# Chunk 0's row tiles shared with GpSimd, the lane one-hots on ScalarE, chunk 2's convolution off VectorE, and a new table of places, in a fused Mamba and mixture-of-experts layer

## The chip, the core and the metric

The kernel runs on one core of a Trainium2 chip. A core has TensorE (PE, matrix multiply), VectorE (DVE), ScalarE (ACT), GpSimd (POOL) and SyncE (SP, which here only issues DMAs). Each engine works through its own list of instructions in order; semaphores tie the lists together. The metric is the device time of one launch in microseconds (us), the median of three runs. A measurement of this kernel tells changes of about 0.2% (2.5 us) from none.

## The reference

The input is 4 sequences of 1024 tokens with 256 features, all float32. It is normalized by a layernorm to `xn`, and three things are added: the input, a Mamba block of `xn`, and a mixture of experts of `xn`.

```
xn    = layernorm(x)
# Mamba: 512 channels, 16 states
rn    = xn * rsqrt(mean(xn^2) + eps) * norm_w
skip, x_in = rn @ skip_w.T, rn @ in_w.T
x     = silu(conv_b + sum_k x_in[t-3+k] * conv_w[:, k])          # 4 taps in time
delta = softplus(x @ wd1.T @ wd2.T + wd2_b)
h[t]  = exp(delta[t] * A) * h[t-1] + delta[t] * x[t] * B[t]      # per channel and state
y[t]  = sum_n h[t, :, n] * C[t, n] + x[t] * W_D
mamba = xn + (y * silu(skip)) @ out_w.T
# experts: the 2 of 8 with the LOWEST gate are used for each token
gates = softmax(xn @ Wr); scores of the two, normalized to sum 1
ffn   = sum_e score_e * ((silu(xn @ W1[e]) * (xn @ V1[e])) @ W2[e])
out   = x + mamba + ffn
```

## The kernel before

**Tiling.** The 4096 tokens are cut into 16 chunks of 256 (`CHUNKS`); four chunks make a sequence. In a chunk the recurrence over time is done state by state: a unit `w` is one chunk, one half `q` of the 512 channels and one of the 16 states, so a chunk has 32 units and the kernel 512. For each unit ACT makes two decays `aexp` (`exps`, L557), DVE makes the product of delta, x and B (`bps`, L1149) and runs two scans along time (`hb`, L1170), and for each pair of units POOL multiplies the states by C (`part`, L775) and PE adds them up over the states by transposing into one accumulator (`yps`, L870). C and B rows come broadcast from DRAM (`bcr`, SP). DVE also saves the last state of each scan (`carry`, L1158). At the start of each half chunk ACT copies x into `ups` (`fill_ups`, L566), and DVE multiplies it by delta (L1142).

**Pieces and places.** All other work is cut into pieces, and a table says in which unit of which chunk each piece stands (`pieces`, `B_PLACES`, `O_PLACES`, `F_PLACES`); `LATER` moves a kind of piece some units back on one engine. Every engine does, in each unit `w`, its own part of the unit and then its part of the pieces at `w`. ACT makes the decays two units ahead (`EXP_AHEAD`). A piece that must wait holds everything behind it on that engine. Pieces that matter here:
- `B1`, `B2`, `CV`/`CW`, `X2`, `B3`, `B4`, `B5`, `SP`, `DL`: the next chunk's x, convolution, delta, and B and C rows. The convolution is either on DVE (`DVE_CONV`, L1294 and L1298) or as `CV` on ACT (four scaled copies, L617 and L619) and `CW` on POOL (two additions, L805 and L807). `DL`, one addition of 128x1024, is on DVE (`DVE_DELTA`) or on POOL. `O1` to `O3`: the end of the chunk before (DVE L1305).
- `R`, 18 pieces in chunk 0: the row tiles. For each pair of the 32 tiles of 128 tokens, ACT writes the normalized rows into one of two buffer pairs `tok` (L688), SP stores them, POOL writes the residual (L797), PE transposes the rows of the pair before (L1006), ACT copies them out of the banks (L694), and PE multiplies the pair before that with the router (L998).
- `RA` to `RE`: the router's softmax, choice and placement, mostly on DVE, one instruction after another. They need all of `R`.
- `M`, 8 rounds in chunk 1: from the slot of each token the lists of the experts' tiles are built. Each round DVE makes a one-hot of the tile (L1279) and one of the lane within it (`hot`, 8 rows of 128, L1282), POOL multiplies (L815, L817), PE adds up 8 products in bank X (L1020). DVE may not overwrite a buffer of two rounds ago before PE has read it (`placed`).
- `MF`: DVE turns bank X into the index list (L1332 to L1336). `FB` -1: POOL gathers the rows of the first two tiles by it (L783), PE transposes the first (L1050), ACT copies it (L715). Then `FA`, `FB`, `FC` are the steps of each of the 71 expert tiles, in chunks 2 to 15: DVE L1340 and L1348, PE L1033, L1057, L1067.

Of the kernel before, what the change touches and what calls it, by code (L numbers as in the profile page):

```python
# [22 lines left out]
P = 128  # L23
# [36 lines left out]
    "other": [4, 6, 7, 8, 11, 11, 12, 14, 14, 16, 16, 18, 21, 23, 23, 24, 25, 26, 26],  # L60
# [5 lines left out]
    1: [1, 4, 4, 11, 18],  # L66
    14: [3, 3, 3, 15, 18],
    15: [0, 0, 6, 7, 15],
# [6 lines left out]
    "five": [1, 6, 8, 10, 13, 15, 16, 16, 17, 19, 20, 28, 29, 29, 30],  # L75
    "six": [0, 0, 5, 9, 10, 11, 11, 14, 15, 17, 17, 19, 26, 26, 28, 29, 29, 31],
# [4 lines left out]
    "router": [8, 8, 8, 9, 9, 9],  # L81
# [4 lines left out]
DVE_CONV = (0, 2)  # L86
# [3 lines left out]
DVE_DELTA = (0, 2)  # L90
# [60 lines left out]
def carry_copies(w):  # L151
# [74 lines left out]
def mamba_moe(nc, x, norm_w, skip_wT, in_wT, conv_w, conv_b, wd1T, wd2T, wd2_b, wBCT, A_log, W_D, out_wT,  # L226
# [3 lines left out]
    with ctx:  # L230
# [132 lines left out]
        added = sem("added")  # L363
        hot_set = sem("hot_set")
# [11 lines left out]
        y_taken = sem("y_taken")  # L376
        xn_r = sem("xn_r")
# [56 lines left out]
        def _(sp):  # L434
# [19 lines left out]
            def do(piece):  # L454
# [17 lines left out]
                elif kind == "R" and piece[1] < TT // 2:  # L472
# [4 lines left out]
                    sp.wait_ge(xn_r, 2 * (i + 1))  # L477
# [5 lines left out]
                elif kind == "R" and piece[1] == TT // 2:  # L483

                    sp.dma_start(v1[:, :].rearrange("p (e k f) -> p e k f", e=EXPERTS, k=KD), V1.rearrange("e (k p) f -> p e k f", p=P)).then_inc(ld_v1, 16)
                    sp.wait_ge(xn_r, TT)
# [50 lines left out]
        def _(act):  # L537
# [38 lines left out]
            def do(piece):  # L576
# [102 lines left out]
                elif kind == "R":  # L679
                    i = piece[1]  # L680
                    if i < TT // 2:
                        if i == 0:
                            act.wait_ge(stat, STAT_LN[1])
                        if i >= 2:
                            wait_full(act, "V", ("R", i - 1))
                            act.wait_ge(xt_out[i % 2], 16 * (i // 2))
                        for t in (2 * i, 2 * i + 1):
                            nc.scalar.activation(tok[:, t % 4, :], xall[:, t, :], ACT.Identity, bias=nm2[:, 0, t:t + 1],  # L688
                                                 scale=rs2[:, 0, t:t + 1]).then_inc(xn_r, 1)
                    if 1 <= i <= TT // 2:  # L690
                        for k, t in enumerate((2 * i - 2, 2 * i - 1)):
                            wait_full(act, "HV"[k], piece)
                            at_least(act, lgt, t - 1)
                            nc.scalar.activation(xT[:, k, :, :], bank["HV"[k]][:, 0:D].rearrange("p (k t) -> p k t", k=KD),  # L694
                                                 ACT.Copy).then_inc(free["HV"[k]], 1)
                elif kind == "RA":
# [58 lines left out]
        def _(pool):  # L755
# [30 lines left out]
            def do(piece):  # L786
                kind = piece[0]
                if kind == "R" and piece[1] < TT // 2:
                    i = piece[1]
                    if i == 0:  # L790
                        pool.wait_ge(stat, STAT_LN[1])
                        for k in range(TT // 8):
                            pool.wait_ge(ld_x[k], 16)
                    at_least(pool, res_out[i % 2], 16 * (i // 2))
# [64 lines left out]
        def _(pe):  # L859
# [30 lines left out]
            def do(piece):  # L890
# [99 lines left out]
                elif kind == "R":  # L990
# [10 lines left out]
                    if 1 <= i <= TT // 2:  # L1001
                        for k, t in enumerate((2 * i - 2, 2 * i - 1)):
                            wait_free(pe, "HV"[k], piece)
                            pe.wait_ge(xn_r, t + 1)
# [82 lines left out]
        def _(dve):  # L1087
# [184 lines left out]
            def value_rows(r):  # L1272
# [7 lines left out]
                if r == 0:  # L1280
                    dve.wait_ge(ones_set, 2)
                v.tensor_tensor(hot[r % 2], steps.unsqueeze(1).to_broadcast([P, ROUND, P]),  # L1282
                                lane[:, at].unsqueeze(2).to_broadcast([P, ROUND, P]), ALU.is_equal).then_inc(hot_set, 1)
# [130 lines left out]
```

## Time and profile before

| | us |
|---|---|
| median of 3 runs (1269.9 to 1270.19) | 1269.93 |
| the profiled execution's own time | 1272.05 |
| its span, first to last instruction | 1270.2 |
| DVE busy in the span | 1173.1 (92%) |
| PE, ACT, POOL busy | 1076.9, 1010.5, 998.2 |
| first scan of chunks 0, 1, 2, 3, 4 starts at | 40.8, 126.4, 246.3, 323.8, 395.4 |

Busy time is the sum over an engine's instructions. The later chunks take about 72 us each; chunk 0 takes 85 us and chunk 1 120 us. "Idle before" in a row is what an engine stood still before the instruction, and the name behind the arrow is what ended it.

### The profile page before, as it was taken

How to read it: one execution, taken by the hardware profiler on the slowest of the kernel's cores; microseconds unless marked ns; L12 is line 12 of the kernel's file. 1: busy time of each engine (PE TensorE's matmuls, PEld its weight loads, DVE VectorE, ACT ScalarE, POOL GpSimd, SP SyncE). 2: the span in 40 equal slices, each digit the busy share in tenths (PEclk: the TensorE clock that was granted, in tenths of full speed). 3: DMA queues.
4: the chain of work that ended last, by engine and by line, in shares of the span. 5: the costliest groups of instructions: out<-in, count | busy, mean ns of one | idle time of the engine just before them, and what ended most of it. 6: DMA issues, size and time to landing. Idle time of an engine off the chain costs nothing.

```text
span 1270.2 us, 20047 instructions
## 1 busy us (share of the span) xinstructions
PE 1076.9 (85%) x5406; PEld 806.6 (64%) x5406; DVE 1173.1 (92%) x2128; ACT 1010.5 (80%) x2151; POOL 998.2 (79%) x601
## 2 busy tenths in 40 slices
PE   4378576498898989999999999999999999998776
PEld 3266475365666666676767766676766667675664
DVE  5976899989999899999999999999999999999896
ACT  4898346379888897889888898889889898987853
POOL 1487176667898988889898998889899898988764
PEclk8686778798999999999999999999999999998977
DMA  7467822644445454555545454555545455544536
GB/s 229 154 200 227 312 82 82 203 162 130 142 141 153 135 148 153 145 149 137 149 133 161 134 161 139 147 148 131 155 139 157 142 150 150 147 134 132 135 128 191
DMA packets 87117, 195.08 MB, mean 154 GB/s; under 512 B 11184, under 2 KB 47152, under 8 KB 86928
## 3 DMA queue, kind: packets, MB, share of 16 engines
q1 hardware_dynamic: 69008, 171.18, 40.7%
q0 software_dynamic: 17712, 22.55, 10.9%
q8 instruction: 47, 0.77, 0.2%
q14 instruction: 62, 0.51, 0.1%
q10 hardware_dynamic: 288, 0.07, 0.0%
HBM read 171.22 MB, written 26.48 MB: 156 GB/s over the span
## 4 chain that ended last, share of the span: by engine, by line
PE 31%; POOL 29%; ACT 14%; issue 13%; DVE 11%; DMA 1%; POOLq 0%; DVEq 0%; ACTq 0%
POOL part L775 15%; PE yps L870 7%; POOL acc L831 5%; POOL tap L805 4%; ACT aexp L557 4%; PE bankX L1067 4%; PE bankH L1033 4%; PE bankV L1057 4%; DVE hb L1170 3%; PE bankG L910 3%; POOL scr L783 2%; ACT L557 2%; DVE bps L1149 2%; PE bankV L910 2%; POOL x L807 2%
## 5 line engine op out<-in xcount | busy, mean ns | idle before, releaser
L775 POOL TENSOR_TENSOR part<-hb,bcr 128x1024 f32<-128x1024 f32 x256 | 618.3, 2429 | 172.4 <-DVE hb L1170 141.2
L1170 DVE TENSOR_TENSOR_SCAN hb<-aexp,carry,bps 128x256 f32<-128x256 f32 x768 | 545.5, 734 | 4.2 <-ACT aexp L557 4.1
L557 ACT ACTIVATE aexp<-delta,Am 128x256 f32<-128x256 f32 x1024 | 446.8, 501 | 53.0 <-DVE hb L1170 42.0
L870 PE MATMUL yps<-idn,part 128*128 128x128 f32 x2048 | 299.8, 286 | 74.1 <-POOL part L775 64.0
L1149 DVE TENSOR_TENSOR bps<-ups,bcr 128x512 f32<-128x512 f32 x512 | 345.8, 675 | 3.4 <-DMA bcr<-brows 2.3
L870 PEld LDWEIGHTS yps<-idn,part 128*128 128x128 f32 x2048 | 249.9, 147 | 151.2 <-POOL part L775 83.0
L1170 DVE TENSOR_TENSOR_SCAN hb<-aexp,bps 128x256 f32<-128x256 f32 x256 | 167.3, 673 | 10.8 <-ACT aexp L557 10.2
L1067 PE MATMUL bankX<-w,scr 128*128 x568 | 138.7, 388 | 10.5 <-ACT scr L715 8.1
L1033 PE MATMUL bankH<-w,scr 128*128 x284 | 136.8, 604 | 2.2 <-issue 1.0
L1057 PE MATMUL bankV<-v,scr 128*128 x284 | 134.2, 595 | 1.2 <-ACT xin L610 0.8
L831 POOL DMA_INDIRECT acc<-scr,idx x71 | 114.2, 1609 | 24.6 <-issue 11.5
L1067 PEld LDWEIGHTS bankX<-w,scr 128*128 128x128 f32 x568 | 105.6, 194 | 28.1 <-issue 15.6
L805 POOL TENSOR_TENSOR tap<-tap 128x512 f32<-128x512 f32 x56 | 84.7, 1513 | 1.0 <-ACT tap L619 1.0
L783 POOL DMA_INDIRECT scr<-xt,idx x71 | 72.2, 1016 | 13.8 <-issue 7.9
L1033 PEld LDWEIGHTS bankH<-w,scr 128*128 128x128 f32 x284 | 50.3, 193 | 40.1 <-issue 39.2
L619 ACT ACTIVATE tap<-xin,cw 128x256 f32<-128x256 f32 x168 | 72.5, 497 | 0.0
L1057 PEld LDWEIGHTS bankV<-v,scr 128*128 128x128 f32 x284 | 48.4, 190 | 36.5 <-issue 35.9
L1340 DVE SCALAR_TENSOR_TENSOR scr<-scr,bankH 128x512 f32<-128x512 f32 x71 | 47.6, 671 | 22.5 <-ACT scr L705 22.5
L557 ACT ACT_TABLE_LOAD x50 | 64.2, 1283 | 0.9
L705 ACT ACTIVATE scr<-bankH 128x512 f32<-128x512 f32 x71 | 41.7, 587 | 28.8 <-PE bankH L1033 28.5
L725 ACT ACTIVATE scr<-bankX,meta 128x256 f32<-128x256 f32 x71 | 33.1, 466 | 38.3 <-PE bankX L1067 38.3
L1040 PEld LDWEIGHTS bankG<-idn,scr 128*128 128x128 f32 x284 | 35.4, 141 | 37.4 <-issue 36.9
(179 smaller groups left out, 1625.1 us busy)
## 6 DMA issues: line engine op xcount, KB each, us to landing
bcr<-brows SPq DMA_DIRECT2D x256, 512.0 KB
w<-in_W SPq DMA_DIRECT2D x2, 4096.0 KB, 22.1
xch<-in_x SPq DMA_DIRECT2D x16, 256.0 KB, 4.5
w<-in_x SPq DMA_DIRECT2D x4, 1024.0 KB, 9.7
xt<-scr SPq DMA_DIRECT2D x16, 256.0 KB, 3.0
acc<-scr SPq DMA_DIRECT2D x16, 256.0 KB, 2.8
v<-in_V SPq DMA_DIRECT2D x1, 4096.0 KB, 16.0
acc<-mst POOLq DMA_DIRECT2D x15, 256.0 KB
```

Source lines behind the costliest of these rows:

```text
L557: nc.scalar.activation(aexp[:, w % EXP_SLOTS, i, :], delta[:, c % 2, e, :], ACT.Exp, scale=Am[:, e, n:n + 1]).then_inc(s_a, 1)
L619: ins = nc.scalar.activation(tap[:, w, :], xin[:, e, w:w + CH], ACT.Copy, scale=cw[:, e, w:w + 1])
L775: nc.gpsimd.tensor_tensor(part[:, slot:slot + 2, :, :], hb[:, state:state + 2, :, :], bcr[:, row:row + 2, CH:2 * CH].unsqueeze(2).to_broad ...
L783: nc.gpsimd.indirect_dma_start(out=tok[:, j % 2, :], out_offset=None, in_=xt, in_offset=bass.IndirectOffsetOnAxis(ap=idx[:, j:j + 1], axis ...
L805: nc.gpsimd.tensor_tensor(tap[:, 0:2, :], tap[:, 0:2, :], tap[:, 2:4, :], ALU.add).then_inc(cvs, 1)
L831: nc.gpsimd.indirect_dma_start(out=acc, out_offset=bass.IndirectOffsetOnAxis(ap=idx[:, j:j + 1], axis=0), in_=tok[:, 2 + j % 2, :], in_off ...
L870: mm = pe.matmul(yps[:, s, i * P:(i + 1) * P], part[:, w % (2 * PART_PAIRS), i, s * P:(s + 1) * P], idn[:, :], start=(n == 0 and s == 0 an ...
L1033: mm = pe.matmul(bank["H"][:, :], xT[:, j % 2, k, :], w1[:, bass.ds(col + k * FF, FF)], start=(k == 0), stop=(k == KD - 1))
L1057: mm = pe.matmul(bank["V"][:, :], xT[:, j % 2, k, :], v1[:, bass.ds(columns[j] + k * FF, FF)], start=(k == 0), stop=(k == KD - 1))
L1067: mm = pe.matmul(bank["X"][:, 0:D], gT[:, k * P:(k + 1) * P], w2[:, bass.ds(columns[j] + k * D, D)], start=(k == 0), stop=(k == FF // P - 1))
L1149: v.tensor_tensor(bps[w % 2][:, :, :], ups[:, :, :], bcr[:, w % (2 * ROW_PAIRS), 0:CH].unsqueeze(1).to_broadcast([P, 2, CH]), ALU.mult).th ...
L1170: v.tensor_tensor_scan(hb[:, w % STATE_SLOTS, i, :], aexp[:, w % EXP_SLOTS, i, :], bps[w % 2][:, i, :], first, ALU.mult, ALU.add).then_inc ...
```

## The change

Three kinds of work move, and the tables of places and of `LATER` have new numbers.
- Of each pair of row tiles ACT normalizes the even one as before, and POOL the odd one, by one `tensor_scalar`, before it writes the residual of the pair. A new semaphore `xn_p` counts POOL's tiles beside `xn_r`; PE and SP wait for both.
- The lane's one-hots are no longer made by one comparison on DVE. ACT makes each round by eight activations `Abs(lane - step)` of 128x128 and, once these are done (`far_set`), one `Relu(1 - ...)` of 128x1024. ACT now waits for the end of the router (`STAT_END`) and for `placed`.
- Chunk 2's convolution goes to ACT (`CV`) and POOL (`CW`), and its `DL` to POOL. Only chunk 0 keeps them on DVE.

```diff
@@ tables (a line or two of each) @@
-    1: [7, 7, 8, 8, 9, 12, 12, 14, 14, 16, 16, 17, 20, 20, 22, 22, 22, 22, 25],
+    1: [6, 6, 8, 9, 9, 9, 11, 11, 11, 11, 12, 15, 21, 22, 22, 22, 27, 27, 27],
...
-    1: [2, 4, 6, 8, 14, 20, 22, 24, 29, 30],
+    1: [2, 4, 6, 8, 10, 20, 22, 24, 31, 31],
...
-    "router": [8, 8, 8, 9, 9, 9],
+    "router": [8, 8, 8, 8, 8, 8],
...
-DVE_CONV = (0, 2)
+DVE_CONV = (0,)
...
-DVE_DELTA = (0, 2)
+DVE_DELTA = (0,)
@@ ScalarE @@
-                        for t in (2 * i, 2 * i + 1):
-                            nc.scalar.activation(tok[:, t % 4, :], xall[:, t, :], ACT.Identity, bias=nm2[:, 0, t:t + 1],
-                                                 scale=rs2[:, 0, t:t + 1]).then_inc(xn_r, 1)
+                        t = 2 * i
+                        nc.scalar.activation(tok[:, t % 4, :], xall[:, t, :], ACT.Identity, bias=nm2[:, 0, t:t + 1],
+                                             scale=rs2[:, 0, t:t + 1]).then_inc(xn_r, 1)
...
+                elif kind == "M":
+                    r = piece[1]
+                    if r == 0:
+                        act.wait_ge(stat, STAT_END)
+                        act.wait_ge(ones_set, 2)
+                    if r >= 2:
+                        act.wait_ge(placed, r - 1)
+                    for k in range(ROUND):
+                        at = r * ROUND + k
+                        ins = nc.scalar.activation(hot[r % 2][:, k, :], steps, ACT.Abs, bias=lane[:, at:at + 1], scale=-1.0)
+                    ins.then_inc(far_set, 1)
+                    act.wait_ge(far_set, r + 1)
+                    nc.scalar.activation(hot[r % 2], hot[r % 2], ACT.Relu, bias=1.0, scale=-1.0).then_inc(hot_set, 1)
@@ GpSimd @@
+                    if i >= 2:
+                        wait_full(pool, "V", ("R", i - 1))
+                        pool.wait_ge(xt_out[i % 2], 16 * (i // 2))
+                    t = 2 * i + 1
+                    nc.gpsimd.tensor_scalar(tok[:, t % 4, :], xall[:, t, :], rs2[:, 0, t:t + 1], nm2[:, 0, t:t + 1],
+                                            ALU.mult, ALU.add).then_inc(xn_p, 1)
@@ TensorE @@
-                            pe.wait_ge(xn_r, t + 1)
+                            pe.wait_ge((xn_r, xn_p)[k], t // 2 + 1)
@@ VectorE @@
-                if r == 0:
-                    dve.wait_ge(ones_set, 2)
-                v.tensor_tensor(hot[r % 2], steps.unsqueeze(1).to_broadcast([P, ROUND, P]),
-                                lane[:, at].unsqueeze(2).to_broadcast([P, ROUND, P]), ALU.is_equal).then_inc(hot_set, 1)
```

ACT's list in chunk 1, behind the router, before the change: from the silu of `O2` 1 (y<-bankV) to the copy of chunk 0's output (mst).

```order
L668 ACTIVATE y<-bankV 128x512
L557 ACT_TABLE_LOAD
L557 ACTIVATE aexp<-delta,Am 128x256 x6
L587 ACTIVATE xch<-xch,nm,rs 128x256 x2
L593 ACTIVATE rnT<-bankG,nw 128x256 x2
L557 ACTIVATE aexp<-delta,Am 128x256 x2
L607 ACTIVATE xin<-xin 128x4x3
L610 ACTIVATE xin<-bankG 128x2x256
L557 ACTIVATE aexp<-delta,Am 128x256 x4
L610 ACTIVATE xin<-bankV 128x2x256
L557 ACTIVATE aexp<-delta,Am 128x256 x2
L678 ACTIVATE mst<-bankH 128x256
```

The end of the same stretch with the change (w<-w are the one-hots' parts, tap<-xin the convolution's `CV`; its lines are numbered a little higher).

```order
L709 ACTIVATE w<-w 128x128 x8
L712 ACTIVATE w<-w 128x1024
L561 ACTIVATE aexp<-delta,Am 128x256 x2
L621 ACTIVATE tap<-xin,cb,cw 128x256
L623 ACTIVATE tap<-xin,cw 128x256 x3
L561 ACTIVATE aexp<-delta,Am 128x256 x2
L614 ACTIVATE xin<-bankV 128x2x256
L709 ACTIVATE w<-w 128x128 x8
L712 ACTIVATE w<-w 128x1024
L561 ACTIVATE aexp<-delta,Am 128x256 x2
L621 ACTIVATE tap<-xin,cb,cw 128x256
L623 ACTIVATE tap<-xin,cw 128x256 x3
```

Up to this copy ACT now has five rounds of one-hots and all four `CV` in its list, between the same decays; it had none of either.

DVE's list around the index list (`MF`: meta and idx) at the end of chunk 1, before the change.

```order
L1332 COPY meta<-bankX 128x71
L1334 TENSOR_SCALAR w<-bankX,idb 128x71
L1336 CAST idx<-w 128x71
L1170 SCALAR_TENSOR_TENSOR hb<-aexp,carry,bps 128x256
L1149 TENSOR_TENSOR bps<-ups,bcr 128x512
L1170 SCALAR_TENSOR_TENSOR hb<-aexp,carry,bps 128x256
L429 TENSOR_TENSOR delta<-delta,y 128x1024
L1158 TENSOR_REDUCE carry<-hb 128x4
L1170 SCALAR_TENSOR_TENSOR hb<-aexp,carry,bps 128x256
L1142 TENSOR_TENSOR ups<-ups,delta 128x512
```

And with the change.

```order
L1193 SCALAR_TENSOR_TENSOR hb<-aexp,carry,bps 128x256
L1165 TENSOR_TENSOR ups<-ups,delta 128x512
L1172 TENSOR_TENSOR bps<-ups,bcr 128x512
L1193 SCALAR_TENSOR_TENSOR hb<-aexp,carry,bps 128x256
L1351 COPY meta<-bankX 128x71
L1353 TENSOR_SCALAR w<-bankX,idb 128x71
L1355 CAST idx<-w 128x71
```

`MF` stood before the last two units of chunk 1 and now stands behind them; `DL` is gone from the list.

## Rows read from the trace of the kernel before

**Rows 1.** Busy time by stage: window, length, PE, PEld, DVE, ACT, POOL busy, clock, DMA.

```profile
49.30:108.40 59.10, 43.98 (x256) 37.08 (x256) 50.27 (x97) 56.27 (x130) 49.12 (x41) 0.80 0.60 195
108.40:131.30 22.90, 20.32 (x93) 18.72 (x94) 7.74 (x13) 16.79 (x39) 12.65 (x15) 0.54 0.73 240
...
155.70:237.20 81.50, 53.53 (x300) 46.58 (x300) 81.03 (x134) 42.30 (x83) 56.58 (x30) 0.82 0.28 86
237.20:264.40 27.20, 15.08 (x62) 11.22 (x62) 19.98 (x35) 12.03 (x24) 12.48 (x7) 0.69 0.80 262
```

**Rows 2.** DVE's waits from 49.3 to 131.3 us: total, times, longest.

```profile
DVE ups L1142 <- ACT ups L566: 10.4, 2, 9.5
DVE hb L1170 <- ACT aexp L557: 8.5, 6, 2.0
```

**Rows 3.** ACT in order of time, chunk 0: start, length in us, instruction.

```profile
53.76 1.08 ACT L688 ACTIVATE scr<-w,nm,rs 128x256 f32<-128x256 f32 x2
54.75 0.36 ACT L694 ACTIVATE scr<-bankH 128x256 f32<-128x256 f32 x1
...
58.19 0.60 ACT L617 ACTIVATE tap<-xin,cb,cw 128x256 f32<-128x256 f32 x1
...
59.90 1.08 ACT L688 ACTIVATE scr<-w,nm,rs 128x256 f32<-128x256 f32 x2
```

**Rows 4.** POOL's residual writes, 49.3 to 131.3 us: busy us, mean ns.

```profile
L797 POOL TENSOR_SCALAR scr<-w,r,nm 128x256 f32<-128x256 f32 x32 | 17.5, 558 | 7.6 <-DMA acc<-scr 5.1 <-DVE r L1130 2.5
```

**Rows 5.** PE in order of time, the last row tiles.

```profile
109.81 1.47 PE L998 MATMUL bankX<-wrt,scr 128*128 128x8 f32 x8 [3.09 <-ACT scr L694]
...
126.03 1.87 PE L998 MATMUL bankX<-wrt,scr 128*128 128x8 f32 x8
129.49 1.72 PE L998 MATMUL bankX<-wrt,scr 128*128 128x8 f32 x8
```

**Rows 6.** DVE in order of time, between the router's two halves.

```profile
140.60 0.43 DVE L1215 TENSOR_TENSOR w<-w 128x256 f32<-128x256 f32 x1
...
143.26 0.42 DVE L1224 COPY w<-bankV 128x256 f32<-128x256 f32 x1
```

**Rows 7.** DVE's groups from 155.7 to 246.3 us: busy us, mean ns.

```profile
L1282 DVE TENSOR_TENSOR w<-w 128x1024 f32<-128x1024 f32 x8 | 9.7, 1215 | 0.0
...
L1298 DVE SCALAR_TENSOR_TENSOR x<-xin,cw,x 128x256 f32<-128x256 f32 x12 | 5.8, 485 | 0.4
L1294 DVE TENSOR_SCALAR x<-xin,cw,cb 128x256 f32<-128x256 f32 x4 | 3.3, 825 | 0.0
```

**Rows 8.** ACT in order of time, two activations of `B4` and one of `SP`.

```profile
215.21 0.47 ACT L650 ACTIVATE delta<-bankH,db 128x256 f32<-128x256 f32 x1
215.57 0.48 ACT L648 ACTIVATE y<-bankH,db 128x256 f32<-128x256 f32 x1
...
219.64 1.04 ACT L657 ACTIVATE y<-y 128x1024 f32<-128x1024 f32 x1
```

**Rows 9.** ACT's decays, 155.7 to 237.2 us: busy, mean ns, idle before.

```profile
L557 ACT ACTIVATE aexp<-delta,Am 128x256 f32<-128x256 f32 x52 | 22.9, 500 | 30.8 <-DVE hb L1170 30.7
```

**Rows 10.** ACT's waits for PE in that window, first and last of seven.

```profile
ACT mst L678 <- PE bankH L957: 6.3, 1, 6.3
...
ACT y L648 <- PE bankH L936: 0.5, 1, 0.5
```

**Rows 11.** DVE, then PE, in order of time, from the index list on.

```profile
237.65 2.12 DVE L1336 CAST idx<-w 128x71 int32<-128x71 f32 x1
...
248.11 0.66 PE L1050 MATMUL bankX<-idn,scr 128*128 128x128 f32 x2 [11.49 <-DMA scr<-xt,idx]
253.28 3.78 PE L1033 MATMUL bankH<-w,scr 128*128 x4
```

**Rows 12.** DVE in order of time, its last long wait in chunk 2.

```profile
300.18 0.69 DVE L1340 SCALAR_TENSOR_TENSOR scr<-scr,bankH 128x512 f32<-128x512 f32 x1 [2.70 <-ACT scr L705]
```

**Rows 13.** DVE's longest waits in total, 395.4 to 1117.6 us.

```profile
DVE scr L1340 <- ACT scr L705: 11.6, 13, 1.8
```

More of the change, by code:

```diff
@@ L56 @@
 B_PLACES = {
[3 rows of a table removed]
-    "other": [4, 6, 7, 8, 11, 11, 12, 14, 14, 16, 16, 18, 21, 23, 23, 24, 25, 26, 26],
[3 rows of a table added]
+    "other": [4, 6, 7, 9, 11, 11, 13, 14, 15, 17, 17, 18, 21, 23, 23, 23, 24, 26, 27],
 }
@@ L65 @@
 O_PLACES = {
-    1: [1, 4, 4, 11, 18],
-    14: [3, 3, 3, 15, 18],
-    15: [0, 0, 6, 7, 15],
+    1: [1, 3, 4, 12, 19],
+    14: [3, 3, 4, 10, 20],
+    15: [0, 0, 5, 6, 11],
     "other": [3, 3, 3, 15, 19],
@@ L71 @@
 F_PLACES = {
[3 rows of a table removed]
-    "five": [1, 6, 8, 10, 13, 15, 16, 16, 17, 19, 20, 28, 29, 29, 30],
-    "six": [0, 0, 5, 9, 10, 11, 11, 14, 15, 17, 17, 19, 26, 26, 28, 29, 29, 31],
[3 rows of a table added]
+    "five": [0, 7, 8, 11, 13, 15, 16, 16, 17, 19, 20, 28, 29, 29, 31],
+    "six": [0, 0, 5, 8, 8, 11, 11, 14, 15, 17, 17, 19, 26, 26, 28, 29, 29, 30],
     15: [17, 21, 29, 29, 31],
@@ L363, in mamba_moe @@
         added = sem("added")
+        far_set = sem("far_set")
         hot_set = sem("hot_set")
@@ L376, in mamba_moe @@
         y_taken = sem("y_taken")
+        xn_p = sem("xn_p")
         xn_r = sem("xn_r")
@@ L476, in do @@
                         sp.dma_start(xt[TOKENS:TOKENS + P, :], empty).then_inc(xt_zero, 16)
-                    sp.wait_ge(xn_r, 2 * (i + 1))
+                    sp.wait_ge(xn_r, i + 1)
+                    sp.wait_ge(xn_p, i + 1)
                     sp.dma_start(xt[2 * i * P:2 * (i + 1) * P, :].rearrange("(s p) d -> p s d", p=P),
@@ L485, in do @@
                     sp.dma_start(v1[:, :].rearrange("p (e k f) -> p e k f", e=EXPERTS, k=KD), V1.rearrange("e (k p) f -> p e k f", p=P)).then_inc(ld_v1, 16)
-                    sp.wait_ge(xn_r, TT)
+                    sp.wait_ge(xn_r, TT // 2)
+                    sp.wait_ge(xn_p, TT // 2)
                     sp.wait_ge(res_set, TT)
```

16 rows, old and new, of tables (B_PLACES, F_PLACES, LATER) are left out of this document.

## The prediction

> **What bounds the kernel now.** I read the profile in this order: busy time by stage, DVE's waits, and then the lists of ACT, POOL and PE in order of time in the stretches that the change touches. From chunk 3 on DVE is the bound: it has 64 scans and 32 products in every chunk, and from 395 to 1118 us its largest wait comes to 11.6 us [rows 13]. The change leaves that part nearly as it is, so its worth is decided before 324 us, in four stretches with four different bounds.
>
> - 49.3 to 108.4 us, chunk 0 behind the row statistics. ACT is busy 56.3 of 59.1 us, POOL 49.1, DVE 50.3 [rows 1]. DVE waits for decays, 8.5 us in this stretch and the next [rows 2]: ACT is the bound.
> - 108.4 to 131.3, the last eight pieces `R`. Nobody is full in the table [rows 1], and DVE stands 9.5 us before the `ups` of chunk 1 [rows 2], which ACT has behind these pieces. From the first to the last of seven PE steps L998 are 19.68 us, so 3.28 us a piece, of which one L998 alone is 1.87 at a granted clock of 0.54, that is mostly the 1.2 GHz level [rows 1, 5]. The bound is the ring PE, ACT, PE.
> - 131.3 to 155.7 the router, on DVE alone; 155.7 to 237.2 the rest of chunk 1 up to `MF`: DVE busy 81.0 of 81.5, ACT 42.3, POOL 56.6 [rows 1]. ACT stands 30.7 us there because DVE has not scanned [rows 9]. DVE is the bound by a wide margin.
> - 237.2 to 264.4, from the index list to the end of chunk 1's `O1` in chunk 2. DVE is busy 20.0 of 27.2 us. It's a chain: list, gather, PE transpose (PE had stood 11.5 us for it), first expert matmul [rows 1, 11].
>
> **Part 1, the row tiles.** Each pair costs ACT 0.99 us from start to start for two tiles [rows 3], so 0.50 for the one that goes. Ten pairs lie in the first stretch: ACT does 5.0 us less there. POOL does 10 tiles more by 0.558 [rows 4], 5.6 us, and comes to 49.1 + 5.6 = 54.7 us of work, where ACT would come to a length of 59.1 - 5.0 = 54.1: the two are level, and each also waits for the other in the convolution. I take 4.0 of the 5.0 us. In the second stretch the tile taken from ACT is beside the ring and not in it; the copy L694 starts some 0.5 us earlier only where the normalization stood ahead of it. The ring without any ACT tile is 1.87 for L998, about 0.7 for the first transposes and 0.4 for the copy, with hand-overs about 3.1 against 3.28: 7 times 0.15 is 1.0 us. Together -5.0. Bounds: all 16 tiles pay at ACT's price, -8.0; POOL becomes the bound, eats the whole gain and adds its own waits, +1.0.
>
> **Part 2, the router in one piece.** `RP` on PE runs between the router's halves. Before, DVE did a whole unit there: from the end of L1215 at 141.03 to L1224 at 143.26 are 2.2 us [rows 6]. All router pieces now stand in one unit, so DVE stands for these 2.2 us, and the unit is still to be done: +2.2, bounds +1.5 and +2.5.
>
> **Part 3, from the router's end to `O1` in chunk 2.** From DVE go 9.7 us of one-hots and 3.3 + 5.8 of convolution [rows 7], and 1.2 of `DL`. To ACT come four `CV`, 1.71 each from start to start [rows 3], 6.8 us, and eight rounds of one-hots, which the trace doesn't show. Their nearest rows are the activations with a bias column on 256 elements: 0.48 long, but started 0.36 apart [rows 8]. For 128 elements I take starts 0.27 apart; 7 of them, one full length of 0.36 before the semaphore lets go, and 1.04 for the 1024 elements of the `Relu`, as in L657 [rows 8], make 3.3 us a round, 26.4 in all. Bounds: if each of the eight takes its whole length, 0.36 each, and 0.1 for the hand-over, a round is 4.0, and all 32; at starts 0.22 apart it is 24.
>
> ACT then has 42.3 us [rows 1], about 2.5 for the decays of two units more that now stand before `MF` (0.88 a unit [rows 9], and a fill), 26.4 and 6.8: 78. It stood 14.5 us for PE in this window, from 6.3 down to 0.5 [rows 10]; most of that was slack and goes when ACT is late itself, and I keep 5. So ACT needs 83.5 us to where `MF` now stands. DVE needs 81.5 - 9.7 - 9.1 + 3.8 for the two units now ahead of `MF` + 1.4 for `ups` and product, 68: it will wait for decays, above all in units 10 to 14, where five rounds and four `CV` stand in ACT's list. POOL gets four `CW` and `DL`, some 10 us: 56.6 + 10 is still below 83.5, and nothing is on the path. Its own wait for ACT holds `parts` behind it, which has slack of two units.
>
> The Trainium skill (ScalarE: Activation LUTs, Rules for kernel authors) budgets about 0.3 us for each activation with a bias column and 0.83 ns an element. By it a round would be 8 times 0.41 and 1.15, 4.4 us, and the eight 35; the case's activations of 256 elements would be 0.51 apart, and they start 0.36 apart [rows 8], so the rule fits a length and not a rate here.
>
> Behind `MF` the chain of 27.2 us [rows 1] stays, but for the sums of PE that had piled up between its transpose and the first expert matmul, 248.77 to 253.28 [rows 11]: `MF` and the gather now come one piece of PE's list later, POOL's products for these sums are then made while PE waits, and I take 2.5 us off. The list's place behind the last two units costs nothing more in this sum, since it is in the 83.5. So before it was 81.5 + 27.2 = 108.7, and now 83.5 + 24.7 = 108.2: -0.5. The 20 us that leave DVE are thus worth almost nothing: ACT is late in their stead, and the chain has two units less of DVE's work to hide behind. Bounds: DVE as the bound, 68 + 24.7, -16; ACT keeping all its 14.5 us of waits, 93 + 24.7, +9.
>
> **Part 4, the rest.** In chunk 2 `FA` 2 stands two units later, and the wait of 2.7 us before it [rows 12] should mostly go: -1.5. In chunks 3 to 15 the places move by one unit here and there; their waits for this step were 11.6 us in ten chunks [rows 13]: 0, with ±2.5.
>
> **The sum.** -5.0 + 2.2 - 0.5 - 1.5 = -4.8. The profiled execution would go from 1272.05 to 1267.2; it was 2.1 above the median of the runs, so the median goes from 1269.93 to **1265.1**.
>
> **The rivals.**
> - *DVE stays the bound in chunk 1* (rounds near 3.0 and no waits of ACT that matter). For it: 30.7 us in which ACT stood [rows 9]. Against it: 33 us are put in, unevenly. -5.0 + 2.2 - 16 - 1.5: 1250.
> - *POOL becomes the bound in chunk 0* and the tiles only change engines. For it: 54.7 against 54.1, and each `R` of POOL now has three steps, with waits for SP's stores before two of them. The -5.0 becomes -1.0: 1269.
> - *Short activations don't overlap*, a round is 4.0. For it only their length [rows 8]; the skill's rule above points the same way, and further. The rounds cost 5.6 more on the bound: 1270.7.
> - *Slower: ACT's waits in chunk 1 don't shrink.* Place: the copies of PE's results by ACT between the router and `MF`. With one-hots in ACT's list, PE's rounds wait for ACT and ACT for PE, and DVE may not start round r before PE has done r-2. Price: 14.5 in place of 5, part 3 is +9, and the sum +4.7: 1274.6. It decides from about 10 us of such waits on, where the sum passes zero. For it: the list is strict, and PE already waited for POOL's rows before. Against it: a late ACT finds PE done.
>
> **Chances.** My forecast, with its own range 1260.5 to 1267.4, 0.45; DVE-bound 0.12; POOL-bound 0.13; no overlap 0.10; slower 0.20. Within 0.2% means 2.5 us, what can't be told from no change. Faster is 0.45 + 0.12 and a little of the third, 0.58; same 0.22; slower 0.20. The range for 8 in 10 reaches over most of both sides: 1253 to 1275.
>
> **What would show it.** Right: ACT nearly full from 155 us to `MF`; DVE with some 12 us of waits for decays there, in units 10 to 14; rounds of 3.3; 2.2 us of DVE standing inside the router; the router's start 5 us earlier; POOL over 90% busy in chunk 0. Wrong: DVE busy all through chunk 1 (first rival); the router's start at 130 (second); Abs starts 0.36 apart or more (third); ACT standing 10 us for PE in chunk 1 (fourth). A change of more than 3 us behind 324 us would mean that the places of the later chunks matter, which I have put at 0.

## The result and the profile after

The changed kernel takes 1262.03 us (median of 4, 1260.95 to 1263.79), the kernel before 1270.06 on the same chip (median of 4): ratio 0.9931, 95% interval 0.9919 to 0.9944, so 8.0 us or 0.7% faster. The profiled spans are 1259.2 and 1270.2, -11.0. The forecast was 1265.1, faster; the time lies in its own range, 1260.5 to 1267.4. Its sum, -4.8, was smaller than the result, and its terms did not all come true.

The changed kernel by stage, in the columns of [rows 1]: row tiles, last pieces `R`, router's end to `MF`, `MF` to the end of `O1` in chunk 2.

```profile
49.30:107.30 58.00, 43.36 (x252) 37.16 (x252) 49.65 (x96) 51.78 (x120) 51.97 (x50) 0.80 0.64 203
107.30:129.80 22.50, 20.34 (x97) 18.93 (x98) 8.67 (x16) 13.76 (x33) 19.03 (x22) 0.57 0.71 230
152.40:236.80 84.40, 54.64 (x316) 46.38 (x316) 71.92 (x122) 78.12 (x179) 65.35 (x41) 0.80 0.30 95
236.80:258.30 21.50, 12.95 (x58) 10.32 (x58) 12.44 (x25) 9.84 (x19) 10.17 (x6) 0.69 0.90 309
```

Against [rows 1] the first stretch is 1.1 us shorter, the second 0.4, the router 1.8 (22.6 for 24.4, between the windows), the third 2.9 longer and the fourth 5.7 shorter. That is -6.1 at the end of `O1`; -4.9 more come behind it.

- **ACT in the first stretch.** Its work fell by 4.5 us, as forecast, but it is no longer nearly full. ACT's waits, and below PE's, from 49.3 to 107.3 (waiter, releaser; total, times, longest):

```profile
ACT y L652 <- PE bankH L959: 2.3, 1, 2.3
ACT xin L614 <- PE bankG L933: 1.5, 1, 1.5
...
PE yps L893 <- POOL part L792: 5.8, 4, 3.3
```

In the same stretch before, ACT's longest wait for PE was 1.0 and PE's for `part` 1.5 in total. DVE's decays cost 11.8 us and the `ups` 2.9 where [rows 2] had 8.5 and 10.4.

- **The router.** DVE in order of time; the place of [rows 6]:

```profile
139.13 0.43 DVE L1238 TENSOR_TENSOR w<-w 128x256 f32<-128x256 f32 x1
141.82 0.42 DVE L1247 COPY w<-bankV 128x256 f32<-128x256 f32 x1 [2.26 <-PE bankV L1037]
142.28 1.11 DVE L1252 TENSOR_TENSOR_SCAN w<-w 128x32 f32<-128x32 f32 x8
```

The wait of 2.2 us is there, 2.26. What I had not seen is the row below it. Before, DVE and then POOL:

```profile
143.72 2.92 DVE L1229 TENSOR_TENSOR_SCAN w<-w 128x32 f32<-128x32 f32 x8
...
143.33 2.35 POOL L775 TENSOR_TENSOR part<-hb,bcr 128x1024 f32<-128x1024 f32 x1 [11.12 <-DVE hb L1170]
```

The first of the eight scans began at 143.72 and took 2.04 us, the other seven 0.20 to 0.21 each. POOL's product ended at 145.68, and there the second scan began. Now no product of POOL stands beside them, and the eight take 1.11.

- **Chunk 1.** ACT in order of time, one round of one-hots, between decays:

```profile
161.44 2.43 ACT L709 ACTIVATE w<-w 128x128 f32<-128x128 f32 x8
163.90 1.06 ACT L712 ACTIVATE w<-w 128x1024 f32<-128x1024 f32 x1
164.87 1.69 ACT L561 ACTIVATE aexp<-delta,Am 128x256 f32<-128x256 f32 x4
```

From 161.44 to 164.87 are 3.43 us. Each `Abs` lasts 0.389 us, by its group of 64, and the eight take 2.43: starts (2.43 - 0.39) / 7 = 0.29 apart. The Trainium skill (ScalarE: Activation LUTs, Rules for kernel authors) budgets 0.3 us and 0.83 ns an element, which gives an estimate of 0.41 us here: the trace agrees with it as a length (0.389), not as a distance between starts.

DVE's and ACT's waits from 152.4 to 236.8:

```profile
DVE hb L1193 <- ACT aexp L561: 5.1, 3, 2.7
DVE hb L1193 <- POOL part L792: 4.5, 1, 4.5
DVE w L1302 <- PE bankX L1043: 1.5, 1, 1.5
...
ACT tap L621 <- POOL x L830: 2.2, 1, 2.2
ACT mst L682 <- PE bankV L980: 1.5, 1, 1.5
```

ACT is busy 78.1 of 84.4 us; just ahead of its first round it stood 4.5 for the end of DVE's router. Of its seven waits for PE [rows 10] those that are left are 1.5 and 0.5. DVE stands 12.4 us, but only 5.1 for decays. The 4.5, up to 193.95, is for a product of POOL. In POOL's list that product stands behind a `CW` (two additions), which had waited 3.9 us for ACT's `CV`:

```profile
189.53 1.26 POOL L828 TENSOR_TENSOR tap<-tap 128x512 f32<-128x512 f32 x1 [3.91 <-ACT tap L623]
190.87 0.72 POOL L830 TENSOR_TENSOR x<-tap 128x256 f32<-128x256 f32 x1
191.55 2.35 POOL L792 TENSOR_TENSOR part<-hb,bcr 128x1024 f32<-128x1024 f32 x1
```

- **From the list to `O1`.** DVE, the `CAST` of [rows 11] and what follows:

```profile
237.29 0.20 DVE L1355 CAST idx<-w 128x71 int32<-128x71 f32 x1
...
246.62 0.75 DVE L1193 TENSOR_TENSOR_SCAN hb<-aexp,carry,bps 128x256 f32<-128x256 f32 x1 [5.21 <-ACT aexp L561]
```

The `CAST` took 2.12 before. The reason is POOL again, before:

```profile
237.37 2.34 POOL L775 TENSOR_TENSOR part<-hb,bcr 128x1024 f32<-128x1024 f32 x1 [1.46 <-DVE hb L1170]
```

It ran to 239.71; the `CAST`, begun at 237.65, ended at 239.77.

- **The later chunks.** DVE's wait for ACT's copy, the group of [rows 13], over the same ten chunks; in chunk 14 what is left of it:

```profile
DVE scr L1359 <- ACT scr L722: 9.1, 11, 1.8
...
DVE scr L1359 <- ACT scr L722: 2.6, 2, 1.4
```

In [rows 13] it was 11.6; in chunk 14 it had been 4.5, with one wait of 3.7 in it. The start of chunk 3 stands at -6.7 against before, of chunk 14 at -8.4, of chunk 15 at -10.8, and the end at -11.0.

### The profile page after: what moved, and what is told of

Same layout as the page of the kernel before. It is cut to its first block, busy times and chain, and to the rows that moved or that the text cites. A ratio compares the mean times of both kernels' runs of the same rounds, so it can differ in the third digit from the quotient of the medians.

```text
span 1259.2 us, 20153 instructions
## 1 busy us (share of the span) xinstructions
PE 1067.6 (85%) x5406; PEld 798.1 (63%) x5406; DVE 1153.9 (92%) x2103; ACT 1035.5 (82%) x2223; POOL 1010.6 (80%) x626
## 4 chain that ended last, share of the span: by engine, by line
PE 33%; POOL 30%; issue 15%; ACT 13%; DVE 6%; DMA 2%; POOLq 0%; DVEq 0%; ACTq 0%; SPq 0%
POOL part L792 16%; PE yps L893 7%; PE bankH L1056 5%; PE bankX L1090 4%; ACT aexp L561 4%; POOL acc L854 4%; PE bankV L1080 4%; POOL tap L828 4%; PE bankG L933 3%; POOL scr L800 2%; PE bankV L933 2%; POOL x L830 2%; ACT L561 2%; DMA acc<-scr,idx 1%; ACT w L709 1%
## 5 line engine op out<-in xcount | busy, mean ns | idle before, releaser
L893 PE MATMUL yps<-idn,part 128*128 128x128 f32 x2048 | 295.3, 285 | 79.6 <-POOL part L792 63.0
L623 ACT ACTIVATE tap<-xin,cw 128x256 f32<-128x256 f32 x180 | 77.7, 496 | 0.0
```

The source lines that it names most:

```text
L623: ins = nc.scalar.activation(tap[:, w, :], xin[:, e, w:w + CH], ACT.Copy, scale=cw[:, e, w:w + 1])
L893: mm = pe.matmul(yps[:, s, i * P:(i + 1) * P], part[:, w % (2 * PART_PAIRS), i, s * P:(s + 1) * P], idn[:, :], start=(n == 0 and s == 0 an ...
```

## The experiments

Ratios are to the kernel before on the same chip; chips differ a little, so ratios are compared, not medians. "Router" is the start of DVE's first read of the logits, "list" the start of the `CAST`; both are from one profile each. Eight of these kernels have the same code and places up to the router, and theirs starts anywhere from 127.8 to 131.0: a difference of 1 or 2 us there, between two profiles, shows little.

| run | ratio (95%) | span | router | router's end to list |
|---|---|---|---|---|
| before | 1 | 1270.2 | 131.3 | 81.9 |
| changed | 0.9931 (0.9919, 0.9944) | 1259.2 | 129.8 | 84.8 |
| places alone | 1.0008 (0.9995, 1.0020) | 1272.5 | 131.6 | 94.2 |
| code alone | 1.0065 (1.0047, 1.0083) | 1277.8 | 131.7 | 92.0 |
| tiles back | 0.9939 (0.9920, 0.9958) | 1263.5 | 131.8 | 84.8 |
| one-hots back | 0.9954 (0.9934, 0.9974) | 1261.7 | 128.1 | 87.9 |
| convolution back | 0.9932 (0.9915, 0.9948) | 1263.8 | 130.1 | 89.2 |
| late places back, `LATER` new | 1.0102 (1.0085, 1.0119) | 1282.2 | 128.2 | 85.0 |
| POOL lighter | 0.9914 (0.9895, 0.9933) | 1258.6 | 129.2 | 84.9 |
| `FA` 0 later | 0.9923 (0.9903, 0.9943) | 1261.0 | 130.8 | 85.2 |
| late chunks back, all | 0.9957 (0.9943, 0.9972) | 1266.7 | 130.8 | 84.9 |
| chunk 14 back | 0.9943 (0.9928, 0.9959) | 1258.3 | 127.8 | 85.0 |
| router in one place | 1.0007 (0.9996, 1.0017) | 1273.6 | 132.1 | 84.4 |
| list early | 0.9899 (0.9881, 0.9918) | 1257.1 | 131.0 | 78.8 |

### The two halves apart

Places alone is the code of before with the changed kernel's tables:

```diff
-    1: [7, 7, 8, 8, 9, 12, 12, 14, 14, 16, 16, 17, 20, 20, 22, 22, 22, 22, 25],
+    1: [6, 6, 8, 9, 9, 9, 11, 11, 11, 11, 12, 15, 21, 22, 22, 22, 27, 27, 27],
...
```

> The code of before with the new tables of places alone: both row tiles of each pair on ACT, one-hots and chunk 2's convolution and DL on DVE. Theory (the places behind 324 us are worth 4.3 us by themselves, and the early places need the new division of work): the first stretch is 3 to 5 us longer than in the changed kernel, since ACT has 8 us of row tiles more and fewer units to hide them; chunk 1 has DVE as the bound with 20 us more on it and two units more before MF, some 5 us longer; chunks 3 to 15 are as in the changed kernel. Median 1266 to 1273. Rival (the places make the whole gain, who does the work is worth nothing): 1261 to 1264.

Code alone is the changed code with the tables of before.

> The new code with the places of before. Theory: half of the row tiles off ACT helps 1 to 3 us in chunk 0; in chunk 1 DVE loses 20 us and ACT gets 33 in places chosen for a free ACT, so the stretch from the router to MF is 78 to 82 us instead of 81.5; chunks 3 to 15 gain nothing (0 against before behind 324 us). Median 1265 to 1270. Rival (the moves of work make the whole gain, the places nothing): 1261 to 1264. If the late chunks gain here all the same, the late places are not what the 4.3 us come from.

Neither half is faster. Places alone is level (1.0008), within the theory and far from the rival. But its stretch in chunk 1 is 94.2 us, 9.4 longer than in the changed kernel, where I had expected some 5. DVE is busy in nearly all of it:

```profile
154.30:248.40 94.10, 53.75 (x316) 46.61 (x316) 92.87 (x148) 45.96 (x91) 62.36 (x32) 0.83 0.28 91
```

Code alone is slower than both theories allowed, by 0.65%: in chunks 1 and 2 DVE stands 27.8 us for decays, since ACT's new work stands in places chosen for an ACT with less to do. In parts of a thousand the halves come to +0.8 and +6.5, the two together to -6.9: most of the gain comes only from both together. Chunk 14 takes 73.4 us with the new places (before and code alone: 75.6), and in both halves no chunk from 4 to 13 differs from before by over 0.6.

### The three moves, taken back one by one

The row tiles:

```diff
-                        t = 2 * i
-                        nc.scalar.activation(tok[:, t % 4, :], ...)
+                        for t in (2 * i, 2 * i + 1):
+                            nc.scalar.activation(tok[:, t % 4, :], ...)
```

> The changed kernel with all sixteen row tiles of chunk 0 on ACT again. In the changed kernel ACT stands for PE in the first stretch (2.25 us at 94.77) and POOL is busy 52.0 of 58.0. Theory (POOL and PE have become the bound of the stretch, the tiles mostly changed engines): the router starts 0 to 2 us later than in the changed kernel, median 1262 to 1264. Rival (ACT is still the bound there, each tile pays 0.5): the router starts 4 to 8 us later, median 1266 to 1270.

The router starts 1.9 us later than in the changed kernel, at the edge of the first theory and far from the rival's 4 to 8. Over all profiles: the four kernels with both tiles on ACT start it at 131.3 to 132.1 (mean 131.7). The eight with the new places and one tile on POOL start it at 127.8 to 131.0 (mean 129.6). That would be 2.1 us, but in three of the eight the granted clock came back ahead of the router (see the last section); the five others start it at 129.8 to 131.0, mean 130.5. So tiles and places are worth between 1.2 and 2.1 us here, and code alone, at 131.7, has none of it. `R` 10 on ACT, ahead of that stretch, starts 1.4 earlier on average in the eight (107.7 for 109.1). The ratio, 0.9939, can't be told from the changed kernel's.

The one-hots:

```diff
-                    for k in range(ROUND):
-                        ins = nc.scalar.activation(hot[r % 2][:, k, :], steps, ACT.Abs, ...)
-                    nc.scalar.activation(hot[r % 2], hot[r % 2], ACT.Relu, bias=1.0, scale=-1.0)
+                v.tensor_tensor(hot[r % 2], steps..., lane[...]..., ALU.is_equal)
```

> The changed kernel with chunk 1's eight rounds of one-hots on DVE again (8 x 1.215 us), ACT without them (8 x 3.43 us). Theory (ACT is the bound of chunk 1's stretch with 77.2 of 82.3 us, DVE has 70.0 in it and 12.3 of waits, so the move has only changed the bound): from the router's end to MF 80 to 83 us against 84.4, median 1259 to 1263. Rival (moving them off DVE is what paid): 88 us and more, median 1266 or above.

My theory fell: 87.9 us, between it and the rival. From 150.7 to 238.6:

```profile
150.70:238.60 87.90, 54.33 (x316) 46.54 (x316) 82.98 (x133) 52.03 (x107) 72.63 (x41) 0.83 0.30 97
```

and DVE's only wait in it:

```profile
DVE hb L1180 <- POOL part L779: 4.8, 1, 4.8
```

DVE became the bound, with 83.0 of 87.9, though it stood no more for ACT. Its wait for POOL stayed, and I had counted those 4.5 us among what would go. In this pair of profiles the stretch is 3.1 us longer, and the ratio, 0.9954, points the same way, though its interval overlaps the changed kernel's.

The move also freed POOL, which neither the forecast nor this expectation had. POOL is busy 72.6 us here against 65.4. All of that is the first of its two products in each round, which is the same instruction in both kernels; this one, then the changed one:

```profile
L825 POOL TENSOR_TENSOR w<-w 128x568 f32<-128x568 f32 x8 | 16.5, 2066 | 5.3 <-DVE w L1289 5.3
L838 POOL TENSOR_TENSOR w<-w 128x568 f32<-128x568 f32 x8 | 9.1, 1143 | 5.1 <-DVE w L1302 5.1
```

With the lane's one-hots on DVE the product begins 0.16 us behind one of them (in seven of the eight rounds) and takes 2.07 us in place of 1.14.

The convolution:

```diff
-DVE_CONV = (0,)
+DVE_CONV = (0, 2)
-DVE_DELTA = (0,)
+DVE_DELTA = (0, 2)
...
-    "DVE": {"FA": 1, "FB": 1, "X2": 4, "O1": 1, "O2": 1, "DL": 3, "CW": 2, "CV": 6},
+    "DVE": {"FA": 1, "FB": 1, "X2": 4, "O1": 1, "O2": 1, "DL": 3},
```

The last pair is of `LATER`: on DVE the convolution stands at its places without a delay. Chunk 0's convolution lies ahead of all units, so this touches chunk 2's alone.

> The changed kernel with chunk 2's four convolutions and its DL on VectorE again; one-hots and places as changed. DVE gets some 10 us in a stretch in which it is busy 70.0 of 82.3, ACT loses 6.8, POOL some 10. Theory (as the run with the one-hots back showed, 9.7 us more on DVE are paid to a third because its waits shrink): router's end to MF 84 to 88 us, median 1263 to 1266. Rival (DVE has 12 us to spare, ACT is the bound, so giving work back to DVE costs nothing or helps): 81 to 84 us, median 1259 to 1262. Second rival (the 4.5 us for which DVE stood for POOL, which had four CW of the convolution in its list, go too): below 81 us.

The stretch is 89.2 us, 4.4 longer than in the changed kernel and just past the first theory's 88, although the 4.5 us for POOL went: DVE is busy 84.2 of 89.1. The ratio, 0.9932, doesn't show these 4.4 us; on the same chip two kernels that differ from the changed one elsewhere had 0.9914 and 0.9923, and the intervals overlap. The profile shows the stretch longer; the times leave it open whether the program is.

### POOL in chunk 0

```diff
-                        nc.gpsimd.tensor_scalar(resid[i % 2][:, k, :], xall[:, t, :], ...)
+                        w = 1 if k and i >= 2 else D
+                        nc.gpsimd.tensor_scalar(resid[i % 2][:, k, 0:w], xall[:, t, 0:w], ...)
```

> The changed kernel, with 14 of GpSimd's 32 residual tiles in chunk 0 cut to one column of 256 (that part of the residual is left out): some 7 us less on POOL, nothing else. Theory (POOL has become the bound of the first stretch with 52.0 of 58.0 us): the router starts 3 to 5 us earlier, median 1257 to 1259. Rival (the bound is the ring PE, ACT, PE behind the tiles, where ACT stood 6.2 us for PE and PE 5.5 for ACT): 0 to 1 us earlier, median 1261 to 1262.

The router starts 0.6 us earlier than in the changed kernel's profile, as the rival has it, and 1.3 earlier than the mean of the five profiles at the same clock. But the dose was smaller than planned. POOL, its tiles of one column:

```profile
L821 POOL TENSOR_SCALAR scr<-w,r,nm 128x1 f32<-128x1 f32 x14 | 4.8, 342 | 0.0
```

A tile of 256 columns is 558 ns, so 14 × 0.216 = 3.0 us went and not 7. With 0.6 to 1.3 us gained of 3.0, the test speaks against POOL as the only bound; it doesn't clear it.

### The router in one place

```diff
-    "router": [8, 8, 8, 9, 9, 9],
+    "router": [8, 8, 8, 8, 8, 8],
```

in the kernel of before, and nothing else.

> The kernel of before with one edit, all six pieces of the router at one place; DVE then has no unit between its product L1215 and the copy L1224. My forecast's step (DVE stands 2.2 us and the unit is still to be done, where DVE is the bound): chunk 1 and the median 2.2 us longer, ratio 1.0017. Theory now (DVE is the bound here, so the 2.2 us are really paid in this kernel, though in the changed one ACT is the bound and hides them; the eight small scans lie 2 us earlier against POOL's product and may keep or lose their 1.8 us): +0.4 to +2.4 us. Rival (nothing is paid, since DVE waits for decays behind the router anyway): within 0.3 us.

DVE, in order of time:

```profile
144.06 0.42 DVE L1224 COPY w<-bankV 128x256 f32<-128x256 f32 x1 [2.26 <-PE bankV L1014]
144.52 1.11 DVE L1229 TENSOR_TENSOR_SCAN w<-w 128x32 f32<-128x32 f32 x8
```

The wait costs 2.26, and the scans, moved away from POOL's product, give 1.81 back. From the router's start to the list are 107.0 us against 106.3: +0.7. The ratio is 1.0007, and its interval, 0.9996 to 1.0017, leaves open both most of the theory's range and the rival's nothing. What is clear is the scans: one edit, POOL's list untouched, and they go from 2.92 to 1.11.

### The late chunks

First the places of chunks 2 to 15 as before, with the delays of `LATER` left new:

```diff
-    "five": [0, 7, 8, 11, 13, 15, 16, 16, 17, 19, 20, 28, 29, 29, 31],
+    "five": [1, 6, 8, 10, 13, 15, 16, 16, 17, 19, 20, 28, 29, 29, 30],
...
```

> The changed kernel with the places that act in chunks 2 to 15 as before; chunks 0 and 1 as changed. Theory (the late places are worth what the profiles differ by behind O1 in chunk 2, 4.3 us, half of it in chunk 14, where the run with the places alone gained 2.2 and the run with the code alone nothing): chunk 14 takes 75.6 us again against 73.2, median 1264 to 1267. Rival (the small differences elsewhere are chance of one profile, and only chunk 14 is real): 1263.5 to 1264.5. Second rival (late places are worth nothing, my forecast's 0): 1261 to 1263.

None of the three: +23 us in the profile. Chunks 5 to 13 take 72.9 to 74.2 us in place of 71.3 to 72.8. From 470 to 1100 us DVE's largest wait is

```profile
DVE scr L1367 <- PE bankV L1080: 12.6, 20, 1.1
```

where the changed kernel has 2.7 in 5. A place and the delay that is added to it are one number in two tables; a mixture tells nothing about either. So both were undone for these chunks:

```diff
+            late = LATER if g < 4 * N else LATER_OLD
-            at[min(g + LATER[engine].get(piece[0], 0), ...)].append(piece)
+            at[min(g + late[engine].get(piece[0], 0), ...)].append(piece)
```

> The changed kernel with everything that sets the order in chunks 2 to 15 as before: the places, and the table of delays (LATER) too, which the former run left new, so that its 23 us belong to a mixture of two tables. Theory (the late places and delays belong together, and behind O1 in chunk 2 the changed kernel gained 4.3 us by them): chunk 14 takes 75.6 us, chunks 3 to 13 as before, median 1264 to 1267, ratio to before 0.996 (0.994 to 0.998). Rival (what was gained there is carried by chance in DVE's short waits): 1262 to 1263, ratio 0.993 to 0.994.

0.9957 against 0.9931, 3.3 us, as the theory has it; the two intervals just touch. Behind the start of chunk 3 this profile loses 5.9 against the changed kernel's: 3.5 in chunk 14 (76.7), 1.5 in chunks 3 to 13, 0.9 in chunk 15. Single profiles scatter here: from the start of chunk 3 to the end, the eight kernels with all the new late places and delays take 1.6 to 4.5 us less than the kernel before (mean 3.3), and the three others with the old ones from 0.9 less to 2.1 more. Of the changed kernel's 4.3, 1.0 is in chunk 9 (71.3 for 72.3), which only one other of the eight has.

Then the lines of places for chunks 14 and 15 alone:

```diff
-    14: [3, 3, 4, 10, 20],
+    14: [3, 3, 3, 15, 18],
...
```

> The changed kernel with the three lines of places for chunks 14 and 15 alone as before. Theory (in chunk 14 the wait of 3.75 us for ACT's copy of a transposed tile at unit 31 is back, in place of 2.6): that chunk takes 75 to 78 us against 73.2, median 1264 to 1267. Rival (the gain of chunk 14 comes from the delays or from the tile places): 73 to 74 us, median 1262.

Chunk 14 takes 75.5 us for 73.2, and DVE stands 5.1 us there for ACT, 3.3 of them at once, where it was 2.6:

```profile
DVE scr L1359 <- ACT scr L722: 5.1, 3, 3.3
```

So chunk 14's places are worth 2.3 us in the profiles: the eight kernels with the new ones take 73.0 to 73.4 us there, the six with the old ones 75.5 and more. The whole program's ratio, 0.9943, is 1.5 us above the changed kernel's and can't be told from it. This profile's span is even shorter, 1258.3, and that is another finding, below.

### Two tries for a faster one

`FA` 0 later:

```diff
-    2: [2, 4, 6, 8, 8, 8, 21, 26, 27, 28, 31, 31],
+    2: [4, 5, 6, 8, 8, 8, 21, 26, 27, 28, 31, 31],
```

> The changed kernel with FA 0 in chunk 2 two places later (4) and FB 0 one later (5). In the changed kernel ACT stands 10.1 us for the transposes of the first gathered tile, which waits for the gather, with the decays behind them in its list, and DVE 5.2 us for these decays; then 1.15, 2.05, 0.61 and 0.95 for the tile and O1. Theory (the list is what makes DVE stand): the 5.2 us go and part of them comes back as a later FA, O1 in chunk 2 ends 2 to 4 us earlier, median 1258 to 1260. Rival (the gather's length sets the time, and the wait only moves): no difference, 1261 to 1263. On the bad side, FB 0 and FC 0 meet O1: 1 to 2 us slower.

No difference, 0.9923. The reason is plain in its profile:

```profile
ACT scr L732 <- PE bankX L1073: 10.6, 1, 10.6
```

The copy that holds up the decays is that of `FB` -1, the transposed first tile, which I had not moved; my expectation named the wrong piece. Moving `FB` -1 itself was not tried.

The list early:

```diff
-    1: [2, 4, 6, 8, 10, 20, 22, 24, 31, 31],
+    1: [2, 4, 6, 8, 10, 20, 22, 24, 29, 31],
```

> The changed kernel with MF in chunk 1 at place 29 for 31 (FB -1 stays), so that DVE writes the index list two units, some 4 us, earlier. Theory (ACT's waits for the gather, 10.1 us, and DVE's 5.2 for the decays behind it shrink by up to 4): O1 in chunk 2 ends 2 to 4 us earlier, median 1258 to 1260. The price: if a product of POOL lies beside it there, the CAST of the list takes about 2 us (2.12 beside POOL's product in the kernel of before, 0.20 with POOL idle); if POOL stands, 0.20. Rival (the sums of PE and FA's copies are bound by ACT's list, not by the list's time): within 0.5 us of 1262.

The theory holds: 0.9899 (0.9881 to 0.9918), 1259.33 us. It is the fastest of all, 1.0% under the kernel before; its interval ends at 0.9918, where the changed kernel's begins (0.9919, on another chip). From the router's start to that of chunk 3 are 184.1 us against 187.3, -3.1. DVE, then POOL, in order of time in this kernel:

```profile
232.47 2.12 DVE L1355 CAST idx<-w 128x71 int32<-128x71 f32 x1
245.17 0.75 DVE L1193 TENSOR_TENSOR_SCAN hb<-aexp,carry,bps 128x256 f32<-128x256 f32 x1 [2.21 <-ACT aexp L561]
251.45 0.70 DVE L1172 TENSOR_TENSOR bps<-ups,bcr 128x512 f32<-128x512 f32 x1 [3.60 <-DMA bcr<-brows]
...
232.19 2.34 POOL L431 TENSOR_TENSOR delta<-delta,y 128x1024 f32<-128x1024 f32 x1 [1.18 <-PE yps L893]
```

and ACT's wait for the transposed first tile:

```profile
ACT scr L732 <- PE bankX L1073: 6.9, 1, 6.9
```

ACT's wait, which hangs on the gather, fell from 10.1 to 6.9, as written down, and DVE's from 5.21 to 2.21. Of the gain, 1.9 went to the `CAST`, which met a product of POOL, and 3.60 to a new wait for the transfer of `bcr`. A place at which POOL is idle, and this load ahead of the gather, would be the next tries; they were not made.

## Why the prediction came out right

Point by point, by its own steps.

- **Part 1, the tiles, -5.0: too much.** The router's start is -1.5 in this pair, -1.2 to -2.1 over all profiles. The step that failed is "ACT does 5.0 us less there. I take 4.0": ACT's work fell by 4.5 us, but its idle time grew from 2.8 to 6.2, of which 5.6 were waits for PE, while PE's for POOL grew from 1.5 to 5.8. ACT had 51.8 us of work and POOL 52.0, not the 54.7 of the forecast, and the stretch still took 58.0. The burst's 1.0 was 0.4. The second rival, "POOL becomes the bound", had the size nearly right, -1.0, but its cause was not shown: 3.0 us less on POOL gave 0.6 to 1.3.
- **Part 2, the router, +2.2: the wait right, the sum wrong.** The wait is 2.26. But the unit "still to be done" falls in chunk 1's stretch, where ACT has more work than DVE, and I had priced that by ACT; where DVE is the bound the single edit costs 0.7 in its profile, after the scans' 1.8. In the changed kernel the router's window is 1.8 shorter. That is 4.0 us from my term, in the good direction.
- **Part 3, -0.5: its first half right, the second short.** Router's end to `MF`: forecast 83.5, measured 84.4; ACT's work 78 and 78.1; a round 3.3 and 3.43; DVE's waits some 12 and 12.4. (The forecast's own terms, 78 and 5, come to 83.0 and not 83.5.) Of DVE's waits 4.5 were for POOL and 1.5 for PE. The step "has slack of two units", for the products of POOL behind its wait for ACT, failed there. From `MF` to the end of `O1`: forecast 24.7, measured 21.5. Of the missing 3.2, 1.9 is the `CAST`; the other 1.3 no run isolates. The claim that the 20 us taken off DVE are "worth almost nothing" holds only against the old program: in the changed one each half, put back, lengthens the stretch, by 3.1 and 4.4 us in the profiles.
- **Part 4, -1.5: wrong by its late half.** The rest of chunk 2 gave -0.6, chunks 3 to 15 -4.3 in the profile (-3.3 on average of the eight), outside ±2.5. The prediction named more than 3 us behind 324 us as the sign of this. The largest part is the single wait of 3.7 us in chunk 14, which stood in the trace of before behind the window of [rows 13] and which I had not read; undone alone, that chunk's places are worth 2.3 us, and all late places with their delays 3.3 by the timed runs.

So the sign was right, and the mechanism in chunk 1 for the most part: work moved from DVE to ACT comes out nearly level there, with ACT close to full. But of the 4.6 us gained from the router's start to the end of `O1`, 3.7 lie in two short pieces of DVE, the scans (1.8) and the `CAST` (1.9), which no longer run beside a product of POOL. No term of the forecast had them.

That the size, -4.8 against -8.0, is near is in part luck, because errors cancel: tiles 3.5 too good; router 4.0, `MF` to `O1` 3.2 and the late chunks 4.3 too bad; chunk 1 and chunk 2's rest 0.9 each too good. 11.5 less 5.3 is 6.2, and -4.8 less 6.2 is the profile's -11.0. The timed runs show 3 us less than the profile.

The rivals: *DVE stays the bound in chunk 1* is refuted (70 to 72 us busy of 84). *Short activations don't overlap* too: starts 0.29 apart, by the sign named for it. *ACT's waits don't shrink* too: 2.0 us for PE, where it needed 10.

## What to carry to other kernels

Read every stretch for its longest single wait, the tail too: the places around one wait of 3.7 us in chunk 14 were worth 2.3 us, about as much as all the row tiles. Compare the length of a small instruction with others of its form: two that were ten times too long made up most of the gain between the router's start and `O1`. An engine with spare time in a sum over a stretch may have none where the work is put, so moved work and its place in the list are priced together: each half of this change alone was level or slower. And a column of places is never undone without the delays that are added to it.

## What the hardware showed beyond that

**DVE behind POOL, and POOL behind DVE.** The same small instructions of DVE have two lengths, by what POOL does beside them. In the fourteen profiles the `CAST` of 71 columns took 2.12 us in four (before, code alone, router in one place, list early) and 0.20 in ten. The eight scans took 2.9 us in two (before, code alone), all of it in the first, and 1.10 to 1.11 in twelve. In all six long cases a product of POOL ran beside them, and the long instruction ended 0.05 to 0.1 us after it: 237.65 + 2.12 = 239.77 against 239.71, and 232.47 + 2.12 = 234.59 against 234.53. In none of the twenty-two short ones did a product run beside them. The Trainium skill (SBUF — State Buffer, SBUF: two separate sides) calls the port pair that the two engines share an exclusive lock between an instruction of GpSimd and one of VectorE in a two-port mode or with two inputs in SBUF. The trace agrees in that each waits for the other's end; in which mode the `CAST` ran it doesn't show. The units' own scans and products have one of their two large inputs in PSUM (`bps`, `ups`), and beside the same products of POOL they are not held up: in the kernel before all 1024 scans take 0.66 to 0.75 us, all 512 products 0.67 to 0.70. The other direction shows in the rounds of one-hots. In the four kernels with the lane's one-hots on DVE, POOL's first product of a round, begun just behind one of them, takes 2.02 to 2.07 us on average and ends about 1.0 us after it; in the ten others it takes 1.14 to 1.20. These costs, 1.9 us twice on DVE and 7 us on POOL, were in the trace of before, as lengths out of line with their forms.

**One stretch, two clocks.** With the same code in chunk 0 (the eight kernels above), the time from `R` 10 on ACT to the router is 22.5 to 22.8 us in five profiles and 20.6 to 20.8 in three. The clock is the third number from the end. The changed kernel:

```profile
119.00:123.00 4.00, 4.00 (x20) 4.00 (x20) 1.15 (x2) 3.41 (x9) 3.67 (x4) 0.50 0.73 236
123.00:127.00 4.00, 3.95 (x19) 3.55 (x20) 3.39 (x6) 1.53 (x4) 4.00 (x5) 0.50 0.83 232
```

Chunk 14 back:

```profile
119.00:123.00 4.00, 4.00 (x21) 4.00 (x19) 1.27 (x2) 3.53 (x9) 3.68 (x4) 0.50 0.92 308
123.00:127.00 4.00, 3.49 (x27) 3.01 (x26) 3.27 (x6) 2.66 (x8) 4.00 (x5) 0.93 0.83 247
```

In the first it stays at 0.50, the level of 1.2 GHz; in the second it comes back to 0.93, nearly that of 2.4, in the last window, as in all three short cases (0.92 to 0.93). PE had been busy in all of the window before in both. What decides is open. It is worth 1.9 us in a profile, more than the row tiles in this pair, so the start of the router is to be compared over several profiles at the same clock.

**A small instruction of POOL.** Its `tensor_scalar` of 128 rows cost 342 ns for one column and 558 for 256 here: making it shorter by 255 columns saves 0.22 us.
